# First and final products of field pairs in one pass of 64 by 32 tiles, and a quad's softmax moved beside the next quad's first fields

## The chip, the cores and the metric

The kernel runs on one core of a Trainium2 chip. The metric is the device time in microseconds (us), as the median of several runs. The engines are TensorE (PE, its weight loads PEld), VectorE (DVE), ScalarE (ACT), GpSimd (POOL) and SyncE (SP). Each follows its own list of instructions in order and waits on semaphores for the others.

## The reference

2048 examples have 26 sparse fields, each an index into a table of 12500 rows of 32 numbers, and 13 dense features. All 325 products of two fields' rows are formed, scored by a small attention layer, and pooled with softmax weights:

```python
emb = jax.vmap(lambda tbl, idx: tbl[idx], in_axes=(0, 1), out_axes=1)(embed_tables, sparse)
bi = emb[:, FIRST, :] * emb[:, SECOND, :]                       # 325 pairs x 32
a = jax.nn.relu(jnp.einsum('bpd,dh->bph', bi, att_w_w) + att_w_b)   # 8 hidden
scores = jnp.einsum('bph,ho->bpo', a, att_d_w) + att_d_b
att_weight = jax.nn.softmax(scores, axis=1)
att_out = jnp.sum(att_weight * bi, axis=1)
x = jnp.concatenate([att_out, dense], axis=-1)
out = jax.nn.sigmoid(x @ fin_w + fin_b)
```

The kernel uses that `att_out @ fin_w` is the softmax-weighted sum over pairs of `bi @ fin_w`. So each pair needs two numbers: a score, and a "final" number `bi @ fin_w`.

## The kernel before

The 2048 examples are 4 quads of 4 x 128. Within a quad the loop runs over fields f = 0 to 25.

POOL fetches field rows with indirect transfers (line 431): 4 for each field (2 for field 24, whose other rows SP fetches; none for fields 3, 9, 15 and 19), 86 for a quad, 344 in all. It may start a field of quad q when field f of quad q - 1 has been transposed (line 425), so it may run up to a quad ahead.

Fields 3, 9, 15 and 19 (`LOOK`) are looked up by PE: DVE makes a one-hot matrix (L750), PE multiplies it with the table held in memory (L465, 14 products), and DVE masks and sums the result (L835, L838). Most fields up to 22 have one such look-up beside them, for this quad or the next; the last quad's stop after field 16.

DVE transposes a field (L826), ACT copies the transposed field to PSUM (L651), and DVE multiplies it with all earlier fields (L850). In the last quad DVE itself writes fields 21 to 25 to PSUM (L824). The pairs go, 16 to a group, through a ring of 4 groups; a quad has 21 groups, numbered 0 to 20 here. Groups 15 and 16 end within field 23, group 17 within field 24, groups 18 to 20 within field 25.

For each group PE makes the first products (L482: 4 column tiles of 32, all 128 rows) and, from the same data, the final products (L492). ACT applies relu (L594). Score products (L506) come in batches that end at groups 3, 7, 11, 15, 17 and 20. Sums of scores and of finals gather for 8 groups in a bank each. Then ACT copies a bank to SBUF (L607, L601), PE turns it back (L530, L522), and ACT brings scores and finals home (L622, L613).

Softmax over the first 256 pairs ("early": maximum L890, exponentials L628, sums L895) is done around fields 24 and 25. The rest ("late") follows at the end of the quad: L905 to L945 on DVE and L682 to L687 on ACT. The next quad's first field comes after it. At the very end come the sigmoid and the store.

Of the kernel before, what the change touches and what calls it, by code (L numbers as in the profile page):

```python
# [6 lines left out]
G = 4  # L7
# [4 lines left out]
GROUPS_B = 8  # L12
ROWS_G = P // GROUPS_B
PAIRS_B = GROUPS_B * PAIRS_G
RING = 4
HIDDEN = 6
BATCH = 4
ROWS_SP = 32
# [17 lines left out]
DMA_SCRATCH = 8192  # L36
DIRECT_LAST = 21
# [3 lines left out]
def layout(n_fields, n_dense):  # L41
    at, cols = 0, {}
    for name, width in (("offset", n_fields), ("w", TILE), ("fin", GROUPS_B * TILE), ("d", 2 * TILE), ("bias_a", 1),
                        ("bias_s", 1), ("dense_w", n_dense), ("fin_b", 1), ("ident", P),
                        ("look_chunk", CHUNKS), ("look_row", CHUNK_ROWS)):
        cols[name] = slice(at, at + width)
        at += width
    return cols, at


def attention_fm(nc, dense, sparse, tables, params, look_index, sp_index, chunk_numbers, out):
# [11 lines left out]
    BANKS = -(-GROUPS // GROUPS_B)  # L63
    FULL = BANKS - 1
    LAST = PAIRS - (GROUPS - 1) * PAIRS_G
    LAST_C = -(-LAST // COL_TILES)
    EARLY_PAIRS = FULL * PAIRS_B
    END_GROUPS = GROUPS - FULL * GROUPS_B
# [31 lines left out]
    SHARED_LAST = next(f for f in range(F) if f * (f + 1) // 2 >= (GROUPS_B + 1) * PAIRS_G) - 3  # L100
    look_bank, shared_through = [], []
    for q in range(QUADS):
        for f in range(F + 1):
            for tile in tiles_beside(q, f):
                look_bank.append(1 if f <= SHARED_LAST and look_bank and look_bank[-1] == 0 else 0)
        shared_through.append(max(tile for tile in range(len(look_bank)) if look_bank[tile]) + 1)

    def taken_before(tile):

        return max([t + 1 for t in range(tile) if look_bank[t] == look_bank[tile]], default=0)  # L110

# [10 lines left out]
    assert G * D == P and B % (P * G) == 0 and RING < GROUPS and 1 < END_GROUPS  # L122
# [17 lines left out]
    def groups_of(f):  # L140
# [5 lines left out]
    batch_ends = [gr for gr in range(GROUPS) if gr == GROUPS - 1 or  # L146
                  gr % BATCH == BATCH - 1 and gr < FULL * GROUPS_B or
                  gr == GROUPS - 4]
    assert groups_of(F - 1) == [GROUPS - 3, GROUPS - 2, GROUPS - 1] and groups_of(F - 2) == [GROUPS - 4]
    BATCHES = len(batch_ends)  # L150

# [3 lines left out]
    def place(gr):  # L155

        return gr % BATCH * 2 + gr % GROUPS_B // BATCH


    EARLY_FIELD = 1 + next(f for f in range(F) if FULL * GROUPS_B in groups_of(f))  # L160
    assert EARLY_FIELD < F - 1

    def pairs_c(gr):
        return PAIRS_C if gr < GROUPS - 1 else LAST_C

# [9 lines left out]
    with ctx:  # L175
# [6 lines left out]
        def sem(name):  # L182
# [25 lines left out]
        look_masked = sb("look_masked", [P, D, CHUNK_ROWS])  # L208
        emb_t = sb("emb_t", [P, COPIES, P])
# [3 lines left out]
        hidden = sb("hidden", [P, HIDDEN, PAIRS_C * P])  # L213
        shared = sb("shared", [P, 2 * PAIRS_C * P + 2 * G * WIDTH])
        second_s, second_f = (shared[:, i * PAIRS_C * P:(i + 1) * PAIRS_C * P] for i in range(2))
        score, final = (shared[:, 2 * PAIRS_C * P + i * G * WIDTH:2 * PAIRS_C * P + (i + 1) * G * WIDTH].rearrange(
            "p (g e) -> p g e", g=G) for i in range(2))


        raw_group = {0: 2, 1: 0, 2: 2}  # L220
        raw = [ring[:, raw_group[n]:raw_group[n] + 2].rearrange("p r c j b -> p (r c j b)")[:, 0:PART_ROWS * D]
               if n in raw_group else shared[:, 0:PART_ROWS * D] for n in range(LOOKS)]
# [4 lines left out]
        wrap, moved = (score[:].rearrange("p g e -> p (g e)")[:, i * T * F:(i + 1) * T * F].rearrange(  # L227
            "p (t f) -> p t f", f=F) for i in range(2))
        index_clamped, index_wrap, index_part = (
            final[0:QUADS * LOOKS * G].rearrange("p g e -> p (g e)")[:, G * P + i * P:G * P + (i + 1) * P] for i in range(3))  # L230
        sp_clamped, sp_wrap = (score[0:T].rearrange("p g e -> p (g e)")[:, i * P:(i + 1) * P] for i in range(2))
# [786 lines left out]
```

## Time and profile before

| | |
|---|---|
| time, median of 3 runs | 464.23 us (463.27 to 464.31) |
| time of the profiled execution | 463.98 us, with a span of 462.1 us |
| busy: PE / DVE / POOL / ACT | 398.6 / 395.8 / 333.7 / 129.8 us |
| mean granted TensorE clock | 0.965 of full |

The span is what the profiler shows between the first and the last instruction. The time holds 1.9 us more. Busy shares are averages over stages with different limits. The chain that ended last runs to 47% over POOL's gathers, and another 19% is "issue", nearly all of it between two gathers.

### The profile page before, as it was taken

To read this page: it belongs to the slowest core of one execution; us is meant where nothing else is said; L and a number is where in the kernel's file an instruction comes from. 1 tells how busy PE (TensorE), PEld (TensorE's weight loads), DVE (VectorE), ACT (ScalarE), POOL (GpSimd) and SP (SyncE) were. 2 spreads that over 40 slices of the span, in tenths; PEclk is the share of its full clock that TensorE was granted. 3 is DMA by queue.
4 is the path that set the end of the run, shared out by engine and by line. 5 is a ranking of instruction groups with operands and counts; after the bars stand their busy time and mean duration, and the time that the engine had idled before them with its cause. 6 is when DMAs were issued, how large, how long until landed. Compare 5 with 4: busy or idle time off the path is not lost.

```text
span 462.1 us, 9274 instructions
## 1 busy us (share of the span) xinstructions
PE 398.6 (86%) x2508; PEld 223.6 (48%) x2508; DVE 395.8 (86%) x641; ACT 129.8 (28%) x302; POOL 333.7 (72%) x350
## 2 busy tenths in 40 slices
PE   1686969998898889599988889699989899699894
PEld 0575736553327656244524757354433666434121
DVE  5999797999796978899796998799977898798995
ACT  3303311232252011033252211114235211124363
POOL 5877777777777777777777777777777777777720
PEclk9988879999999999899999999889999999989999
DMA  8467322222112323222212232313211223322210
GB/s 288 99 152 161 28 13 26 17 26 15 14 14 14 37 15 26 14 21 20 18 15 13 26 25 27 14 16 25 16 14 16 15 14 16 13 16 12 17 7 1
DMA packets 16308, 15.44 MB, mean 33 GB/s; under 512 B 7952, under 2 KB 15360, under 8 KB 15872
## 3 DMA queue, kind: packets, MB, share of 16 engines
q0 software_dynamic: 11072, 5.69, 22.9%
q1 hardware_dynamic: 2800, 6.79, 4.2%
q10 hardware_dynamic: 2384, 2.37, 1.7%
q8 instruction: 20, 0.33, 0.3%
q14 instruction: 32, 0.26, 0.2%
HBM read 14.79 MB, written 0.02 MB: 32 GB/s over the span
## 4 chain that ended last, share of the span: by engine, by line
POOL 47%; issue 19%; DVE 15%; PE 14%; DMA 3%; ACT 1%; DVEq 0%; ACTq 0%
POOL emb L431 47%; DVE ring L850 9%; PE first L482 4%; PE sums_f L492 3%; PE looked_own L465 3%; DMA emb<-tables,rows 3%; PE sums_s L506 2%; PE back L465 2%; DVE onehot L750 2%; DVE emb_t L826 1%; DVE look_masked L835 1%; DVE emb L838 1%; DMA ids<-sparse 0%; PE back L530 0%; POOL emb_placed L420 0%
## 5 line engine op out<-in xcount | busy, mean ns | idle before, releaser
L431 POOL DMA_INDIRECT emb<-tables,rows x300 | 283.4, 945 | 91.5 <-issue 90.3
L850 DVE TENSOR_TENSOR ring<-emb_t,turned 128x512 f32<-128x512 f32 (+9 forms) x180 | 191.7, 1100 | 0.3
L465 PE MATMUL looked_own<-look_parts,onehot 128*128 128x448 f32 x546 | 125.7, 383 | 8.7 <-DVE look_masked L835 4.0
L465 PEld LDWEIGHTS looked_own<-look_parts,onehot 128*128 128x128 f32 x546 | 104.3, 196 | 38.4 <-issue 17.7
L482 PE MATMUL first<-ring,par 128*32 128x512 f32 (+1 forms) x672 | 89.0, 607 | 29.7 <-DVE ring L850 29.2
L594 ACT ACTIVATE hidden<-first,par 128x512 f32<-128x512 f32 (+1 forms) x84 | 56.5, 677 | 180.6 <-PE first L482 180.1
L465 PE MATMUL back<-look_parts,onehot 128*128 128x448 f32 x350 | 80.3, 382 | 11.1 <-DVE onehot L750 5.2
L492 PE MATMUL sums_f<-ring,par 128*32 128x512 f32 (+1 forms) x672 | 89.6, 601 | 0.0
L465 PEld LDWEIGHTS back<-look_parts,onehot 128*128 128x128 f32 x350 | 66.4, 195 | 30.8 <-issue 13.3
L750 DVE TENSOR_TENSOR onehot<-chunk_of,turned 128x896 fp32r<-128x896 f16 x60 | 63.2, 1053 | 0.0
L826 DVE STREAM_TRANSPOSE emb_t<-emb 128x128 f32<-128x128 f32 x100 | 29.9, 302 | 35.5 <-DMA emb<-tables,rows 19.7
L431 POOL DMA_INDIRECT emb<-tables,rows_first x44 | 48.2, 1096 | 16.4 <-issue 13.1
L651 ACT ACTIVATE turned<-emb_t 128x128 f32<-128x128 f32 x92 | 25.6, 279 | 103.3 <-DVE emb_t L826 99.5
L482 PEld LDWEIGHTS first<-ring,par 128*32 128x32 f32 x672 | 15.2, 109 | 74.9 <-DVE ring L850 61.8
L492 PEld LDWEIGHTS sums_f<-ring,par 128*32 128x32 f32 x672 | 22.4, 113 | 50.3 <-issue 49.4
L838 DVE TENSOR_REDUCE emb<-look_masked 128x32 f32<-128x448 f32 x64 | 39.7, 620 | 2.2
L506 PE MATMUL sums_s<-hidden,par 128*32 128x512 f32 (+1 forms) x168 | 28.0, 657 | 0.0
L835 DVE TENSOR_TENSOR look_masked<-looked_own,look_mask 128x448 f32<-128x448 f32 x39 | 23.9, 612 | 1.3 <-PE looked_own L465 1.3
L835 DVE TENSOR_TENSOR look_masked<-back,look_mask 128x448 f32<-128x448 f32 x25 | 15.3, 611 | 0.4 <-PE back L465 0.4
L905 DVE COPY shared<-sums_f 128x512 f32<-128x512 f32 x4 | 2.8, 692 | 13.4 <-PE sums_f L492 13.4
L506 PEld LDWEIGHTS sums_s<-hidden,par 128*32 128x32 f32 x168 | 4.9, 117 | 13.8 <-issue 7.2
L756 DVE TENSOR_TENSOR look_parts<-ring,look_parts 128x1792 fp32r<-128x1792 f32 (+1 forms) x6 | 10.5, 1786 | 1.2 <-ACT look_parts L576 1.2
(75 smaller groups left out, 134.9 us busy)
## 6 DMA issues: line engine op xcount, KB each, us to landing
emb_placed<-tables SPq DMA_DIRECT2D x768, 0.1 KB
emb<-tables,rows POOLq DMA_INDIRECT x300, 3.3
ring<-tables SPq DMA_DIRECT2D x2, 1568.0 KB, 7.8
shared<-tables SPq DMA_DIRECT2D x1, 1568.0 KB
chunk_of<-chunk_numbers ACTq DMA_DIRECT2D x12, 128.0 KB, 2.9
ring<-tables SPq DMA_DIRECT2D x1, 896.0 KB, 6.0
emb<-tables,rows_first POOLq DMA_INDIRECT x44, 3.1
ring<-tables SPq DMA_DIRECT2D x1, 672.0 KB, 7.4
```

The lines of the kernel that those rows point to most:

```text
L431: pool.indirect_dma_start(emb[:, f, g * D:(g + 1) * D], None, stacked, bass.IndirectOffsetOnAxis(ap=row, axis=0), element_offset=at,).then ...
L465: mm = nc.tensor.matmul(looked_rows[look_bank[tile]], onehot[:, tile % ONEHOTS, c, :], look_parts[:, n, c, k, :], start=c == 0 and k == 0, ...
L482: mm = nc.tensor.matmul(first[gr % 2][j * TILE:(j + 1) * TILE, 0:n * P], w, ring[:, gr % RING, 0:n, j, :], start=True, stop=True)
L492: mm = nc.tensor.matmul(sums_f[j * TILE:(j + 1) * TILE, 0:pairs_c(gr) * P], row, ring[:, gr % RING, 0:pairs_c(gr), j, :], start=e == 0, st ...
L506: mm = nc.tensor.matmul(sums_s[tile * TILE:(tile + 1) * TILE, cut], d_sel[:, half, :], hidden[:, gr % HIDDEN, cut], start=half == 0, stop= ...
L594: nc.scalar.activation(hidden[:, gr % HIDDEN, cut], first[gr % 2][:, cut], ACT.Relu, bias=par[:, cols["bias_a"]]).then_inc(relu_done, 1)
L651: nc.scalar.activation(turned[f % 2][:, 0, :], emb_t[:, f, :], ACT.Copy).then_inc(turned_made, 1)
L750: nc.vector.tensor_tensor(onehot[:, tile % ONEHOTS], numbers.unsqueeze(1).broadcast_to(shape), here.unsqueeze(2).broadcast_to(shape), ALU. ...
L826: tr = nc.vector.transpose(emb_t[:, f, :], emb[:, f, :])
L835: nc.vector.tensor_tensor(look_masked[:], looked_rows[look_bank[tile]].rearrange("p (i d) -> p d i", d=D), mask, ALU.mult).then_inc(look_m ...
L838: nc.vector.tensor_reduce(emb[:, LOOK[n], g * D:(g + 1) * D], look_masked[:], AX.X, ALU.add).then_inc(look_summed, 1)
L850: nc.vector.tensor_tensor(slot[:, at:at + n, :], emb_t[:, i:i + n, :], turned[f % 2][:, 0, :].unsqueeze(1).broadcast_to((P, n, P)), ALU.mu ...
```

## The change

Each group now gets one set of products, L463 of the new kernel, in place of L482 and L492. The 128 rows are split in two halves of 64 (`ROW_TILES = 2`), and for each of the 4 column tiles there is a product for each half. The 32 columns of a tile hold, for the two of the four blocks that lie in that half, the 8 hidden numbers, the final number and its negative. Both go through relu, and the score products then take relu(x) - relu(-x) for the final. One group thus fills two PSUM banks of three (`FIRST_BANKS = 3`) and needs two relus.

Scores and finals land in one bank `sums`, batch by batch. ACT copies it out, PE turns it back into the same bank, and ACT brings scores and finals home. The next batch's score products wait for that. The ring has 3 groups instead of 4, and the hidden buffer 5 instead of 6. The early maximum of quads 0 to 2 stands behind field 25. The late maximum, the early sums and the late sums of a quad stand beside fields 2, 3 and 6 of the next. The last quad has an order of its own.

```diff
-RING = 4
-HIDDEN = 6
+ROW_TILES = 2
+ROWS_T = P // ROW_TILES
+RING = 3
+HIDDEN = 5
 BATCH = 4
+FIRST_BANKS = 3
...
+LATE_MAX_FIELD, EARLY_SUMS_FIELD, LATE_SUMS_FIELD = 2, 3, 6
+LATE_HOME_FIELD, LATE_EXP_FIELD = 3, 4
...
                 def first_products(gr):
                     pe.wait_ge(pieces_done, q * PIECES + pieces_through_group(gr))
-                    if gr >= 2:
-                        pe.wait_ge(relu_done, q * GROUPS + (gr - 1))
...
+                    if unit(q, gr, ROW_TILES - 1) >= FIRST_BANKS:
+                        pe.wait_ge(relu_done, unit(q, gr, ROW_TILES - 1) - FIRST_BANKS + 1)
                     n = pairs_c(gr)
                     for j in range(COL_TILES):
...
+                        for r in range(ROW_TILES):
+                            rows_r = slice(r * ROWS_T, (r + 1) * ROWS_T)
+                            mm = nc.tensor.matmul(
+                                first[unit(q, gr, r) % FIRST_BANKS][j * TILE:(j + 1) * TILE, 0:n * P],
+                                weights[rows_r],
+                                ring[rows_r, gr % RING, 0:n, j, :], start=True, stop=True)
...
                 def score_products(batch):
...
+                    groups = batch_groups(batch)
+                    pe.wait_ge(relu_done, unit(q, groups[-1], ROW_TILES - 1) + 1)
+                    if q or batch:
+                        pe.wait_ge(final_done, q * BATCHES + batch)
+                        pe.wait_ge(score_done, q * (BATCHES - 1) + batch)
...
+                    for r in range(ROW_TILES):
+                        for e, gr in enumerate(groups):
+                            cut = slice(0, pairs_c(gr) * P)
+                            mm = nc.tensor.matmul(sums[e * TILE:(e + 1) * TILE, cut], d_sel[:, r, :],
+                                                  hidden[:, gr % HIDDEN, r, cut], start=r == 0, stop=r == ROW_TILES - 1,
+                                                  skip_group_check=True)
...
+                def turn_back(batch):
+                    pe.wait_ge(second_done, q * BATCHES + (batch + 1))
                     for c in range(PAIRS_C):
...
+                        mm = nc.tensor.transpose(back[:, c, :], second[batch % 2][:, c * P:(c + 1) * P], ident)
+                    mm.then_inc(back_done, 1)
...
+                    if last and gr == GROUPS - 3:
+                        score_products(BATCHES - 2)
+                        turn_back(BATCHES - 2)
+                    first_products(gr)
...
+                    if q == QUADS - 1 and f == EARLY_FIELD:
+                        copy_second(BATCHES - 2)
+                        homes(BATCHES - 2)
+                        exponentiate_early()
...
+                    if q and f == LATE_MAX_FIELD:
+                        late_maximum(q - 1)
+                    if q and f == EARLY_SUMS_FIELD:
+                        early_sums(q - 1)
+                    if q and f == LATE_SUMS_FIELD:
+                        late_sums(q - 1)
```

PE at the end of the last quad, before: from the products of group 15 on. `first` are first products, `sums_f` finals, `sums_s` scores, and `back` (at the end `first` from `shared`) what is turned back.

```order
L482 MATMUL first<-ring,par 32x512 x4
L522 MATMUL back<-par,shared 128x128 x4
L506 MATMUL sums_s<-hidden,par 32x512 x4
L492 MATMUL sums_f<-ring,par 32x512 x4
L530 MATMUL back<-par,shared 128x128 x4
L482 MATMUL first<-ring,par 32x512 x4
L492 MATMUL sums_f<-ring,par 32x512 x4
L506 MATMUL sums_s<-hidden,par 32x512 x2
L482 MATMUL first<-ring,par 32x512 x4
```

These rows begin with group 16; group 15's pair of rows reads like the two ahead of them. The same place in the new kernel, from the products of groups 14 and 15 (x16) to the end:

```order
L463 MATMUL first<-ring,weights 32x512 x16
L480 MATMUL sums<-hidden,par 32x512 x8
L488 MATMUL sums<-par,shared 128x128 x4
L463 MATMUL first<-ring,weights 32x512 x16
L480 MATMUL sums<-hidden,par 32x512 x4
L488 MATMUL sums<-par,shared 128x128 x4
L463 MATMUL first<-ring,weights 32x512 x16
L463 MATMUL first<-ring,weights 32x256 x8
L480 MATMUL sums<-hidden,par 32x512 x2
```

Batches 3 and 4 (the fourth and the fifth) are each scored and turned back before PE goes on to the next group. Before, one turning back of each kind and batch 3's scores stood between groups 16 and 17, batch 4 (the x2) was scored ahead of group 18, and its turning back came together with batch 5's, behind group 20.

ACT at the same place before, from group 17's relu on: the relus write `hidden`, L628 are the early exponentials, L607 copies out the last scores.

```order
L594 ACTIVATE hidden<-first,par 128x512
L628 ACTIVATE shared,early<-shared,neg_max_early 128x256 x4
L594 ACTIVATE hidden<-first,par 128x512 x2
L594 ACTIVATE hidden<-first,par 128x256
L607 ACTIVATE shared<-sums_s,par 128x512
```

And in the new kernel, from the relus of groups 16 and 17 (x4) on, where L564 copies a bank out and L570 and L576 bring scores and finals home:

```order
L557 ACTIVATE hidden<-first,par 128x512 x4
L564 ACTIVATE shared<-sums,par 128x512
L570 ACTIVATE shared<-sums 128x128
L576 ACTIVATE shared<-sums 128x128
L588 ACTIVATE shared,early<-shared,neg_max_early 128x256 x4
L557 ACTIVATE hidden<-first,par 128x512 x4
L557 ACTIVATE hidden<-first,par 128x256 x2
L564 ACTIVATE shared<-sums,par 128x512
```

The early exponentials and all relus of groups 18 to 20 now stand behind the copy and the homecoming of batch 4.

## Rows read from the trace of the kernel before

**Rows 1.** The page, part 1: busy us of each engine, share, instructions.

```profile
PE 398.6 (86%) x2508; PEld 223.6 (48%) x2508; DVE 395.8 (86%) x641; ACT 129.8 (28%) x302; POOL 333.7 (72%) x350
```

**Rows 2.** Groups by line and form, POOL: busy, mean ns, idle before and its releasers.

```profile
L431 POOL DMA_INDIRECT emb<-tables,rows x300 | 283.4, 945 | 91.5 <-issue 90.3 <-DVE emb_t L826 1.2
...
L431 POOL DMA_INDIRECT emb<-tables,rows_first x44 | 48.2, 1096 | 16.4 <-issue 13.1 <-DVE rows_first L701 3.3
```

**Rows 3.** Timeline of POOL at its end: start, us, engine, line.

```profile
434.09 0.94 POOL L431 DMA_INDIRECT emb<-tables,rows  x1 [0.30 <-issue]
...
441.59 0.94 POOL L431 DMA_INDIRECT emb<-tables,rows  x1 [0.30 <-issue]
```

**Rows 4.** Chain that ended last, in order of time: start, us, what.

```profile
399.14 4.00 DMA emb<-tables,rows
```

**Rows 5.** Waits of DVE between 360 and 462 us: total, times, longest.

```profile
DVE emb_t L826 <- DMA emb<-tables,rows: 4.8, 4, 1.9
DVE emb_t L826 <- ACT turned L651: 2.9, 4, 1.1
```

**Rows 6.** Timeline of DVE around the start of the last quad.

```profile
352.65 0.42 DVE L895 CUSTOM_DVE_ANT_0 shared<-shared 128x256 f32<-128x256 f32 x1
...
359.04 0.69 DVE L905 COPY shared<-sums_f 128x512 f32<-128x512 f32 x1 [3.92 <-PE sums_f L492]
...
365.18 0.31 DVE L826 STREAM_TRANSPOSE emb_t<-emb 128x128 f32<-128x128 f32 x1 [0.35 <-ACT turned L651]
```

**Rows 7.** Timeline of DVE in the last quad's fields 23 to 25.

```profile
438.44 0.32 DVE L824 STREAM_TRANSPOSE turned<-emb 128x128 f32<-128x128 f32 x1
...
446.56 1.22 DVE L890 TENSOR_REDUCE neg_max_early<-shared 128x4 f32<-128x1024 f32 x1 [0.37 <-ACT shared L622]
...
448.04 3.62 DVE L850 TENSOR_TENSOR ring<-emb_t,turned 128x512 f32<-128x512 f32 x3
```

**Rows 8.** Timeline of PE there.

```profile
439.58 1.07 PE L482 MATMUL first<-ring,par 128*32 128x512 f32 x8 [0.88 <-DVE ring L850]
...
443.36 1.07 PE L506 MATMUL sums_s<-hidden,par 128*32 128x512 f32 x8
444.24 1.04 PE L492 MATMUL sums_f<-ring,par 128*32 128x512 f32 x8
...
450.98 1.50 PE L482 MATMUL first<-ring,par 128*32 128x512 f32 x16 [0.27 <-DVE ring L850]
...
455.08 0.66 PE L530 MATMUL back<-par,shared 128*128 128x128 f32 x4 [0.37 <-ACT shared L607]
```

**Rows 9.** Timeline of ACT there.

```profile
440.71 0.69 ACT L594 ACTIVATE hidden<-first,par 128x512 f32<-128x512 f32 x1 [1.97 <-PE first L482]
...
447.81 0.51 ACT L628 ACTIVATE shared<-shared,neg_max_early 128x256 f32<-128x256 f32 x1 [0.17 <-DVE neg_max_early L890]
...
449.92 0.69 ACT L594 ACTIVATE hidden<-first,par 128x512 f32<-128x512 f32 x1
452.12 1.05 ACT L594 ACTIVATE hidden<-first,par 128x512 f32<-128x512 f32 x2 [1.51 <-PE first L482]
454.34 0.69 ACT L607 ACTIVATE shared<-sums_s,par 128x512 f32<-128x512 f32 x1 [1.17 <-PE sums_s L506]
```

**Rows 10.** Groups by line and form.

```profile
L482 PE MATMUL first<-ring,par 128*32 128x512 f32 x640 | 87.3, 618 | 29.7 <-DVE ring L850 29.2
L492 PE MATMUL sums_f<-ring,par 128*32 128x512 f32 x640 | 86.3, 612 | 0.0
...
L506 PE MATMUL sums_s<-hidden,par 128*32 128x512 f32 x160 | 28.0, 670 | 0.0
...
L651 ACT ACTIVATE turned<-emb_t 128x128 f32<-128x128 f32 x92 | 25.6, 279 | 103.3 <-DVE emb_t L826 99.5 <-DVE ring L850 3.4 <-issue 0.3
...
L594 ACT ACTIVATE hidden<-first,par 128x256 f32<-128x256 f32 x4 | 1.9, 465 | 0.0
```

**Rows 11.** Timeline of PE after an idle stretch in the last quad.

```profile
404.91 1.21 PE L482 MATMUL first<-ring,par 128*32 128x512 f32 x8 [4.03 <-DVE ring L850]
```

More of the change, by code:

```diff
@@ L497, in score_products @@
-                def score_products(batch):
-                    first_gr, end = batch_ends[batch - 1] + 1 if batch else 0, batch_ends[batch]
-                    n = first_gr // GROUPS_B
-                    pe.wait_ge(relu_done, q * GROUPS + (end + 1))
-                    if first_gr % GROUPS_B == 0 and n:
-                        pe.wait_ge(second_s_done, q * BANKS + n)
-                    for gr in range(first_gr, end + 1):
-                        tile, half = place(gr) // 2, place(gr) % 2
-                        cut = slice(0, pairs_c(gr) * P)
-                        mm = nc.tensor.matmul(sums_s[tile * TILE:(tile + 1) * TILE, cut], d_sel[:, half, :],
-                                              hidden[:, gr % HIDDEN, cut], start=half == 0,
-                                              stop=half == 1 or gr >= FULL * GROUPS_B, skip_group_check=True)
-                    mm.then_inc(scores_done, 1)
@@ L618, in finals_home, with homes @@
+                def finals_home(batch):
+                    groups = batch_groups(batch)
+                    whole = len(groups) - (batch == BATCHES - 1)
+                    mv = nc.scalar.activation(pairs_of(final_all, groups[0], whole), in_bank(1, slice(0, whole)), ACT.Copy)
+                    if batch == BATCHES - 1:
+                        mv = nc.scalar.activation(end_pairs(final_all), in_bank(1, whole)[:, 0:LAST_C], ACT.Copy)
                     mv.then_inc(final_done, 1)
-                def scores_home(n):
-                    act.wait_ge(back_s_done, q * BANKS + (n + 1))
-                    nc.scalar.activation(pairs_of(score, n * GROUPS_B, GROUPS_B), scores_in_bank(every),
-                                         ACT.Copy).then_inc(score_done, 1)
+                def homes(batch):
+                    scores_home(batch)
+                    finals_home(batch)
@@ L893, in _ @@
-                for g in range(G):
-                    dve.wait_ge(early_exp_done, q * G + (g + 1))
-                    nc.vector.tensor_tensor_reduce(
-                        out=expd[:, g, 0:EARLY_PAIRS], in0=expd[:, g, 0:EARLY_PAIRS],
-                        in1=final[:, g, 0:EARLY_PAIRS], scale=1.0, scalar=0.0, op0=ALU.mult, op1=ALU.add,
-                        accum_out=early[:, 1, g:g + 1]).then_inc(early_num_done, 1)
+                    before = []
+                    if f == 1:
+                        before = tiles_beside(q, 0)[-1:] if q == 0 else tiles_beside(q - 1, F)
+                    elif f:
+                        before = tiles_beside(q, f - 1)
@@ L939, in _ @@
[L939 to L945 removed]
+            early_sums(QUADS - 1)
```

414 lines of the change are left out of this document (193 added, 221 removed).

## The prediction

> **What bounds the kernel now.** The page first: PE and DVE are both at 86% [rows 1], which invites the thought that taking products from PE must pay. The groups by line say otherwise. POOL's 300 later gathers have 283.4 us of work and 91.5 us of gaps, and nearly all of the gaps is "issue": only 1.2 us in all is a wait for another engine [rows 2]. One gather starts every 0.945 + 0.30 = 1.25 us, and 344 of them fill the run to 442.5 us (441.59 + 0.94) [rows 3], of a span of 462.1. So POOL is never held by DVE. An earlier DVE doesn't make POOL earlier.
>
> How closely does the rest follow POOL? The chain shows 4.00 us from the start of a field's last gather to its landing (field 14) [rows 4]. The last gather of field 23 starts at 434.09 [rows 3], so it lands at about 438.1. DVE takes up field 23 at 438.44 [rows 7], 4.35 us after that start. In between DVE has waited for gathers 4 times for 4.8 us in the last quad, and for ACT's copy 2.9 us [rows 5]. So whatever DVE, PE and ACT save in quads 0 to 2 is given back to these waits, and field 23 can come at most 0.3 us sooner. What is left for the change to move is the last 23 us.
>
> **What the change does ahead of that.** PE: it loses 86.3 us of final products [rows 10]. The first products stay at 4 column tiles of 512 columns for each row half. If the halves run beside each other, a group still costs 0.88 us (443.36 to 444.24, one set to the next [rows 8]). Score products double, +28.0 us [rows 10]. PE's sum falls to about 340 us. No row shows two row halves together. The bounds are 0.88 us a group (beside each other) and 1.76 (in turn). I take the first, since four column tiles do share the 0.88 us here. The Trainium skill, "TensorEngine Tiling (Array Packing)", Tiling Modes, lists eight independent tiles of 64 by 32, which would give the same. Its section PSUM Bottleneck warns that a tiled TensorE moves the load to whoever empties PSUM. The trace has nothing on that for row halves; here it means the doubled relus, which stand in the sum below by rows.
>
> ACT: 84 more relus at the 0.585 us pace of back-to-back ones add about 49 us, to some 180 of 462. It has room, but its place in the chain grows.
>
> DVE at the quad changes: before, from the end of field 25's products (352.65) to the third transpose of the next quad (365.18) it took 12.5 us, with 3.92 us of waiting for the finals and 0.35 for ACT in it [rows 6]. The softmax steps that move to fields 2, 3 and 6 are the same work elsewhere, and one bank copy of 0.69 goes. What counts is the waiting. Afterwards DVE waits there for ACT's first copy, which stands behind the end of PE's and ACT's chain. By the parts below that is, from the end of field 25's products: groups 19 and 20 through relu, with the homes of batch 4 between, 3.6; scores 1.95; bank copy 0.7; exponentials 2.1; the copy itself 0.3; in all 8.65. The early maximum of 1.22 [rows 7] lies under it at least, so DVE waits 7.4 us at most, against 4.3. Less the 0.69, it comes at most 2.4 us later to the next fields. The cover is the 4.8 us for which it waits for gathers in the last quad [rows 5]. So I cost this at nothing; without the cover it would be 2.4 us, and once only, as the last quad alone decides the end.
>
> Ring of 3: DVE fills a group in 2.3 us (3.62 for 25 pairs [rows 7], so 0.145 a pair) and may be two ahead of PE, which needs 0.88 us for a group and has more idle time than before. Cost nothing; if it costs some tenths in a field, the gather waits cover them up to field 14.
>
> **The last 23 us, step by step.** Parts: first products to their relu 1.13 (439.58 to 440.71 [rows 8, 9]); a pair of relus 0.585 + 0.69 = 1.28 (the row of 1.05 is one of 512 and one of 256 columns, and the latter is 0.465 [rows 9, 10]); scores of a batch, two passes, 0.88 + 1.07 = 1.95 [rows 8]; bank copy 0.69 [rows 9]; turning back 0.66 [rows 8]; hand-overs 0.03 to 0.05 (454.34 + 0.69 to 455.08 [rows 8, 9]); a home of 128 columns 0.28, as a copy of that size [rows 10], and 0.18 for the next behind it; four early exponentials 2.11 (447.81 to 449.92 [rows 9]).
>
> Group 15 is complete when it was before, since field 23 is: its products start at 439.58.
>
> - Relu pair of 15: 440.71 to 441.99. Scores of batch 3: 442.04 to 443.99. Copy to 444.71, turned back at 445.42. PE does nothing else meanwhile, as its order puts this ahead of group 16, whose pairs lie ready.
> - Group 16 at 445.42, relus 446.55 to 447.83, the first done at 447.24. Group 17 needs that bank: 447.29, relus 448.42 to 449.70.
> - Scores of batch 4: 449.75 to 451.70 (two column tiles at a time, same pace). Copy to 452.42, turned back at 453.13, scores and finals home at 453.61. Then the exponentials, to 455.72. Before, they began at 447.81 [rows 9].
> - Only now ACT comes to relu 18: 455.72, first of the pair done at 456.41. Group 19 at 456.46, relus from 457.59, first done 458.28. Group 20 at 458.33; its 256 columns take 0.62 (1.50 for two sets less 0.88 [rows 8]); its relus 459.0 to 459.84.
> - Scores of batch 5: 459.89 to 461.84, copy to 462.56, turned back at 463.27.
>
> Before, the scores were turned back at 455.74 (455.08 + 0.66 [rows 8]) and the span ended 6.4 us later. The new tail behind that point is the same but for a copy of 128 columns in place of 256, 0.1 us less. So the span becomes 463.27 + 6.3 = 469.5, 7.4 us more, and the profiled time 463.98 + 7.4 = 471.4. The median of 464.23 lies 0.25 above the profiled run; I say 471.5.
>
> DVE isn't what holds this up. Its products of field 25 end at about 451.3 instead of 451.66 (448.04 + 3.62 [rows 7]), as batch 3's scores are home at 445.8, so that the wait of 0.37 ahead of the early maximum goes. That gain of 0.35 us lies beside the chain and is worth nothing.
>
> **The rivals.**
>
> *The row halves run in turn.* The groups 15, 16, 17, 19 and half of 20 in the chain each cost 0.88 more: +3.9, 475.4 us. PE's sum would be 427 us (340 and 87.3 [rows 10]) and the quad changes could add to it. For it: no row shows the halves together. Against it: column tiles do overlap.
>
> *The clock falls in the tail.* After 4.03 us of idle PE, one set took 1.21 us instead of 1.07, in a stretch where the granted clock was at the lower level for a part [rows 11]. The new chain leaves PE waiting for ACT for 2 us and more at a time. If the lower level (1.2 GHz) holds from 456 on, the steps of PE double: 0.9 + 0.6 + 1.95 + 0.6, +4 us, 475.5. Against it: the idle stretches are shorter than 4 us.
>
> *Not slower.* The first 44 gathers take 1.096 us on average, the later ones 0.945 [rows 2]: 6.6 us in which POOL is held, all in the prologue while DVE splits the looked-up tables. The change puts these tables elsewhere and DVE's operations may shift against the gathers. If all of this went, POOL's whole schedule would come 6.6 us earlier, and the end too, 464.8, within measuring. It decides from about 6 us on. Against it: the same eight splittings stand in the same order, so I expect it to move by 1 us either way at most.
>
> *DVE doesn't catch up by field 14.* If the quad change costs 3 us more than counted, field 23 comes up to 2 us late, 473.5.
>
> **How the numbers follow.** The chain as written 0.64, with its own range 469.5 to 473.5 (0.5 us for hand-overs on some twenty steps, 1 us for POOL's floor either way). Halves in turn 0.09, clock 0.10, not caught up 0.07. Not slower 0.10, be it by the prologue or by a tail that I read wrongly. What a measurement of this kernel can tell from no change is 0.3%, or 1.4 us. To be faster by more than that the end would have to come before 462.8: with field 25's last gather at 441.59 and 4 us to land, and then its products and the old tail, the old span could shrink by 2 us at best. So faster 0.04, same 0.06, slower 0.90. The range of 467.5 to 475.7 leaves out the not slower case and the far side of the first two rivals.
>
> **What would show it.** In the new profile: POOL's last gather within 1 us of 441.6; a set of eight first products of 1.1 us, not 2; relu 18 behind the early exponentials at about 455.7, though its products lay ready; batch 3's and batch 4's bank copies at about 444 and 451.7; PE idle between them; DVE waiting for scores at the end for some 8 us. Wrong would be: a POOL that ends much earlier or later, DVE waiting for ACT's copies in every field, or first products of twice the length.

## The result and the profile after

The new kernel takes **480.6 us** (median of 4 runs, 478.55 to 481.8), the kernel before on the same chip 463.75 (463.19 to 464.31). The ratio is 1.0362, 95% interval 1.0341 to 1.0382. It was forecast to be slower, at 471.5 with a range of 467.5 to 475.7. The sign is right and the size isn't: 16.9 us lost where 7.3 were forecast.

The profiled execution took 481.23 us, of which 479.4 are the span. First the page's busy times, the slices of the granted clock, and the groups of the lines that the change touches, the parts that answer to [rows 1, 2, 10]:

```profile
PE 375.4 (78%) x2676; PEld 214.9 (45%) x2676; DVE 399.4 (83%) x638; ACT 185.2 (39%) x414; POOL 334.3 (70%) x350
...
PEclk9888979998799899998799899998799899987576
...
L416 POOL DMA_INDIRECT emb<-tables,rows x300 | 284.8, 949 | 91.5 <-issue 89.7
...
L463 PE MATMUL first<-ring,weights 64*32 64x512 f32 (+1 forms) x1344 | 101.6, 663 | 56.2 <-DVE ring L831 40.2
...
L480 PE MATMUL sums<-hidden,par 128*32 128x512 f32 (+1 forms) x336 | 58.8, 733 | 7.1 <-ACT hidden L557 7.1
...
L845 DVE CUSTOM_DVE_ANT_0 shared<-shared 128x256 f32<-128x256 f32 x16 | 9.0, 609 | 6.5 <-ACT shared L588 6.3
L588 ACT ACTIVATE shared<-shared,neg_max_early 128x256 f32<-128x256 f32 x16 | 11.8, 747 | 0.0
L838 DVE TENSOR_REDUCE neg_max_early<-shared 128x4 f32<-128x1024 f32 x4 | 8.3, 2084 | 1.9 <-ACT shared L570 1.9
```

POOL has the same work and the same gaps. PE has lost 23 us of busy time, less than the 59 forecast (398.6 to 340), and the slices say why in part: the granted clock is below full in far more of them, and at the end it stands at 5 to 7 tenths. The last three rows hold something that the forecast had not: the early softmax's own operations are longer, though their shapes are the same.

Next PE's timeline from the products of group 14 on, to be held against [rows 8]:

```profile
436.88 1.09 PE L463 MATMUL first<-ring,weights 64*32 64x512 f32 x16 [0.35 <-ACT hidden L557]
439.93 1.10 PE L463 MATMUL first<-ring,weights 64*32 64x512 f32 x16 [1.96 <-DVE ring L831]
442.46 3.64 PE L480 MATMUL sums<-hidden,par 128*32 128x512 f32 x16 [1.43 <-ACT hidden L557]
446.91 1.11 PE L488 MATMUL sums<-par,shared 128*128 128x128 f32 x4 [0.81 <-ACT shared L564]
447.95 1.96 PE L463 MATMUL first<-ring,weights 64*32 64x512 f32 x16
450.85 1.96 PE L463 MATMUL first<-ring,weights 64*32 64x512 f32 x16 [0.94 <-ACT hidden L557]
454.23 3.63 PE L480 MATMUL sums<-hidden,par 128*32 128x512 f32 x8 [1.42 <-ACT hidden L557]
458.64 0.66 PE L488 MATMUL sums<-par,shared 128*128 128x128 f32 x4 [0.79 <-ACT shared L564]
459.23 1.09 PE L463 MATMUL first<-ring,weights 64*32 64x512 f32 x16
463.41 1.09 PE L463 MATMUL first<-ring,weights 64*32 64x512 f32 x16 [3.09 <-ACT hidden L557]
465.43 1.11 PE L463 MATMUL first<-ring,weights 64*32 64x256 f32 x16 [0.93 <-ACT hidden L557]
467.52 3.63 PE L480 MATMUL sums<-hidden,par 128*32 128x512 f32 x12 [0.98 <-ACT hidden L557]
471.95 0.66 PE L488 MATMUL sums<-par,shared 128*128 128x128 f32 x4 [0.81 <-ACT shared L564]
```

The order is the forecast one, step for step, and from group 15's relu on PE is idle for ACT alone. The same operation stands here at two durations: a group's products (each of the 8 leaves two records, so x16) in 1.09 and in 1.96 us, turning back in 0.66 and in 1.11. All three score batches run at the long one, 3.63 us, where 1.95 was forecast. ACT in the same stretch, to be held against [rows 9]:

```profile
441.15 1.27 ACT L557 ACTIVATE hidden<-first,par 128x512 f32<-128x512 f32 x2 [1.67 <-PE first L463]
...
446.17 0.69 ACT L564 ACTIVATE shared<-sums,par 128x512 f32<-128x512 f32 x1 [3.76 <-PE sums L480]
...
457.90 0.69 ACT L564 ACTIVATE shared<-sums,par 128x512 f32<-128x512 f32 x1 [3.73 <-PE sums L480]
...
459.67 0.77 ACT L588 ACTIVATE shared<-shared,neg_max_early 128x256 f32<-128x256 f32 x1
...
462.59 1.25 ACT L557 ACTIVATE hidden<-first,par 128x512 f32<-128x512 f32 x2
```

The last row is relu 18. Its products ended at 460.32, and it starts when the early exponentials are through, as forecast, but at 462.59 instead of 455.72. The clock, stretch by stretch, in the kernel before (columns: stretch, its us, busy us and instructions of PE, PE's weight loads, DVE, ACT and POOL, granted clock, DMA share, GB/s):

```profile
425.00:441.00 16.00, 13.56 (x120) 3.03 (x112) 15.25 (x18) 5.34 (x11) 12.04 (x14) 1.00 0.28 15
441.00:458.00 17.00, 14.21 (x122) 4.45 (x114) 14.00 (x30) 10.12 (x27) 1.23 (x2) 1.00 0.06 4
```

and in the new kernel:

```profile
425.00:441.00 16.00, 11.59 (x116) 2.21 (x116) 13.95 (x16) 8.39 (x17) 12.05 (x13) 0.78 0.27 15
441.00:458.00 17.00, 12.26 (x64) 2.34 (x60) 11.34 (x11) 5.24 (x10) 1.88 (x2) 0.50 0.10 5
458.00:472.00 14.00, 7.55 (x65) 1.86 (x65) 2.46 (x8) 7.88 (x18) 0.00 (x0) 0.76 0.00 0
```

Between 441 and 458 the new kernel's TensorE runs wholly at the lower level, 1.2 of 2.4 GHz. It was granted the upper one for all of this in the kernel before.

**Where the time went.** Span 479.4 against a forecast of 469.5, 9.9 us more, of which some 0.3 lie in hand-overs and not in this table:

| term | forecast | measured | more |
|---|---|---|---|
| start of the chain, relu 15 | 440.71 | 441.15 | 0.44 |
| three batches' scores | 3 x 1.95 | 3.64, 3.63, 3.63 | 5.0 |
| groups 16, 17, 20, products to relu | 1.13, 1.13, 0.67 | 2.07, 2.06, 1.20 | 2.4 |
| turning batch 3 back | 0.66 | 1.11 | 0.45 |
| four early exponentials | 2.11 | 2.92 | 0.8 |
| last turning back to the end | 6.3 | 6.8 | 0.5 |

The second to fourth terms, 7.9 us, are the lower clock. The last two, 1.3 us, are the softmax's durations.

DVE's rows tell what it did meanwhile, field 23's first transpose, the early maximum, field 25's products and the wait at the end:

```profile
438.79 0.33 DVE L805 STREAM_TRANSPOSE turned<-emb 128x128 f32<-128x128 f32 x1 [1.25 <-DMA emb<-tables,rows]
...
448.48 1.98 DVE L838 TENSOR_REDUCE neg_max_early<-shared 128x4 f32<-128x1024 f32 x1 [1.94 <-ACT shared L570]
450.73 3.62 DVE L831 TENSOR_TENSOR ring<-emb_t,turned 128x512 f32<-128x512 f32 x3
...
472.65 0.29 DVE L854 COPY shared<-sums 128x128 f32<-128x128 f32 x1 [9.30 <-PE sums L488]
```

Field 23 comes at 438.79, against 438.44 before, and DVE stands idle for 9.3 us at the end.

### The profile page after: what moved, and what is told of

It is laid out like the page before. It is cut to its first block, busy times and chain, and to the rows that moved or that the text cites. A ratio compares the mean times of both kernels' runs of the same rounds, so it can differ in the third digit from the quotient of the medians.

```text
span 479.4 us, 9758 instructions
## 1 busy us (share of the span) xinstructions
PE 375.4 (78%) x2676; PEld 214.9 (45%) x2676; DVE 399.4 (83%) x638; ACT 185.2 (39%) x414; POOL 334.3 (70%) x350
## 4 chain that ended last, share of the span: by engine, by line
DVE 32%; PE 25%; POOL 17%; issue 14%; ACT 7%; DMA 3%; another core or an unknown queue 1%; DVEq 0%; POOLq 0%; ACTq 0%
POOL emb L416 17%; DVE ring L831 14%; PE first L463 10%; PE sums L480 8%; DVE onehot L731 7%; PE looked L446 5%; DVE look_masked L816 4%; ACT hidden L557 3%; DMA emb<-tables,rows 2%; ACT shared L588 2%; DVE emb_t L807 2%; DVE emb L819 1%; DVE shared L845 1%; PE sums L488 1%
## 5 line engine op out<-in xcount | busy, mean ns | idle before, releaser
L446 PE MATMUL looked<-look_parts,onehot 128*128 128x448 f32 x896 | 207.9, 389 | 25.1 <-DVE onehot L731 16.6
L446 PEld LDWEIGHTS looked<-look_parts,onehot 128*128 128x128 f32 x896 | 175.6, 201 | 74.1 <-issue 35.9
L557 ACT ACTIVATE hidden<-first,par 128x512 f32<-128x512 f32 x168 | 104.7, 674 | 155.2 <-PE first L463 154.6
L463 PE MATMUL first<-ring,weights 64*32 64x512 f32 (+1 forms) x1344 | 101.6, 663 | 56.2 <-DVE ring L831 40.2
L480 PE MATMUL sums<-hidden,par 128*32 128x512 f32 (+1 forms) x336 | 58.8, 733 | 7.1 <-ACT hidden L557 7.1
L463 PEld LDWEIGHTS first<-ring,weights 64*32 64x32 f32 x1344 | 16.6, 109 | 102.5 <-DVE ring L831 73.3
L816 DVE TENSOR_TENSOR look_masked<-looked,look_mask 128x448 f32<-128x448 f32 x64 | 39.1, 611 | 0.2
L480 PEld LDWEIGHTS sums<-hidden,par 128*32 128x32 f32 x336 | 12.0, 127 | 51.6 <-issue 33.0
L564 ACT ACTIVATE shared<-sums,par 128x512 f32<-128x512 f32 x24 | 16.5, 688 | 34.4 <-PE sums L480 30.6
L488 PE MATMUL sums<-par,shared 128*128 128x128 f32 x96 | 16.0, 290 | 2.4 <-ACT shared L564 2.4
L838 DVE TENSOR_REDUCE neg_max_early<-shared 128x4 f32<-128x1024 f32 x4 | 8.3, 2084 | 1.9 <-ACT shared L570 1.9
L576 ACT ACTIVATE shared<-sums 128x256 f32<-128x256 f32 (+1 forms) x24 | 8.5, 353 | 1.2 <-DVE shared L855 1.2
```

What stands on the lines that cost most here:

```text
L446: mm = nc.tensor.matmul(looked_rows[tile % 2], onehot[:, tile % ONEHOTS, c, :], look_parts[:, n, c, k, :], start=c == 0 and k == 0, stop=c ...
L463: mm = nc.tensor.matmul(first[unit(q, gr, r) % FIRST_BANKS][j * TILE:(j + 1) * TILE, 0:n * P], weights[rows_r], ring[rows_r, gr % RING, 0: ...
L480: mm = nc.tensor.matmul(sums[e * TILE:(e + 1) * TILE, cut], d_sel[:, r, :], hidden[:, gr % HIDDEN, r, cut], start=r == 0, stop=r == ROW_TI ...
L488: mm = nc.tensor.transpose(back[:, c, :], second[batch % 2][:, c * P:(c + 1) * P], ident)
L557: nc.scalar.activation(hidden[:, gr % HIDDEN, r, cut], first[unit(q, gr, r) % FIRST_BANKS][:, cut], ACT.Relu, bias=par[:, cols["bias_a"]]) ...
L816: nc.vector.tensor_tensor(look_masked[:], looked_rows[tile % 2].rearrange("p (i d) -> p d i", d=D), mask, ALU.mult).then_inc(look_masked_d ...
```

## The experiments

Twelve kernels ran. Each median below goes with its ratio to the kernel before, run beside it. In the diffs, `q == QUADS - 1` is the last quad.

**The new kernel once more.** Its runs spread over some 3 us, so it ran again, unchanged, beside three of the others.

> The changed kernel once more, unchanged, on the chip of the three kernels beside it. Theory: 480.6 within its own spread of about 3 us, which comes from when the lower clock level falls; the profiled run shows at least 10 us of the lower level after 425 us. Rival (the chip or the moment made the 480.6): below 475.

Measured 482.22 us (476.43 to 483.23), ratio 1.0358 (1.0286 to 1.0431). The result holds. PE's rows of its profile have the lower clock in three more places:

```profile
440.01 1.96 PE L463 MATMUL first<-ring,weights 64*32 64x512 f32 x16 [2.79 <-DVE ring L831]
...
459.58 1.11 PE L488 MATMUL sums<-par,shared 128*128 128x128 f32 x4 [0.79 <-ACT shared L564]
460.63 1.96 PE L463 MATMUL first<-ring,weights 64*32 64x512 f32 x16
```

So where the lower level begins and ends differs from run to run, and a spread from 476 to 483 us can come from that: of the eight runs the two shortest, 476.43 and 478.55, have the highest mean granted clock, 0.910 and 0.909, against 0.892 to 0.904 in the others.

**The exponentials later.** This undoes the one step of the order by which ACT's early exponentials stand ahead of relu 18.

```diff
                     if q == QUADS - 1 and f == EARLY_FIELD:
                         copy_second(BATCHES - 2)
                         homes(BATCHES - 2)
-                        exponentiate_early()
...
+                if q == QUADS - 1:
+                    exponentiate_early()
                 copy_second(BATCHES - 1)
```

> One edit to the changed kernel, in the last quad only: the early exponentials stand on ScalarE behind the relus of groups 18 to 20 instead of ahead of them. Theory (the last quad's chain runs through every step of PE and ScalarE in turn): the exponentials held relu 18 for 2.9 us in the changed kernel (459.67 to 462.59); now they lie beside batch 5's scores, which took 3.6 us. So 480.6 - 2.9 = 477.7 us. Rival (VectorE or the gathers set the end, and ScalarE's order is beside it): 480.6, no change.

Measured 479.19 (476.24 to 480.4), ratio 1.0312 (1.0278 to 1.0346): 1.4 us less than the new kernel's first median and 3.0 less than its second. PE's last rows of its profile:

```profile
458.07 1.09 PE L463 MATMUL first<-ring,weights 64*32 64x512 f32 x16 [0.94 <-ACT hidden L557]
460.09 1.03 PE L463 MATMUL first<-ring,weights 64*32 64x256 f32 x16 [0.93 <-ACT hidden L557]
462.06 3.63 PE L480 MATMUL sums<-hidden,par 128*32 128x512 f32 x12 [0.94 <-ACT hidden L557]
466.49 1.11 PE L488 MATMUL sums<-par,shared 128*128 128x128 f32 x4 [0.81 <-ACT shared L564]
```

Relu 18 did start at 457.24, behind its own products and not behind exponentials, and the last turning back is at 466.49 instead of 471.95. This one execution has a span of 474.4, 5.0 less, with a granted clock of 0.84 from 441 to 458. Its mean granted clock is 0.913; the other three executions have 0.899 and take 478.52 to 480.4. The step of the order is as forecast, but its price can't be told apart from where the lower level falls.

**PE kept busy.** The looked-up rows' products of tile 0 are made again and again in the last quad, into a bank that nobody reads by then. The output is whole. The first version puts many of them in, 6 behind the products of groups 9 to 18 and 2 or 3 behind the other steps of the chain.

```diff
+                def fill(n):
+                    if q == QUADS - 1:
+                        for c in range(n):
+                            nc.tensor.matmul(looked_rows[0], onehot[:, 0, c, :], look_parts[:, 0, c, 0, :],
+                                             start=True, stop=True)
...
                         first_products(gr)
+                        if gr >= 9:
+                            fill(6)
...
```

> The changed kernel with products that nobody reads, 2 to 6 of 448 columns at a time, put on PE in the last quad from group 9 on, at the places where PE waits for ScalarE. Theory (what the end took beyond the forecast is TensorE's lower clock level): the granted clock stays at the upper level from 440 to 472 us, the scores of a batch take 1.95 us instead of 3.6, the first products of groups 16 and 17 1.1 instead of 1.96, and the time falls by about 8 us, to 472.6. Rival (the row halves and the two passes are slow by themselves, for instance from changing the tiling): the durations stay and the filler adds up to 1 us a batch, 481 to 484.

Measured 475.3 (473.99 to 476.7), ratio 1.0238 (1.021 to 1.0265). The granted clock was 1.00 from 441 to 458 and the scores took 1.91 us, but the filler stood in the way: relu 15 came at 443.77, and the time is 2.7 us above the 472.6 expected. Hence a second version, with 3 at most places and 2, 4 or 6 at three.

> The changed kernel with fewer unread products than in the first filler run, 2 to 6 at a time, sized so that each set ends before PE's next input is there. Theory (the lower level costs some 8 us of the tail, and the first filler run gave back 3 us by standing in the way): relu 15 starts at about 441.3, the clock stays at the upper level in the tail, 472 to 473.5 us. Rival (5 us is all that the clock was worth): 475 or more.

Measured 474.25 (473.16 to 474.86), ratio 1.0221 (1.0194 to 1.0248): 6.4 us less than the new kernel's first median and 8.0 less than its second, which ran beside it. It is a little above the 472 to 473.5 expected. PE's rows in the chain, the filler left out:

```profile
443.18 1.92 PE L486 MATMUL sums<-hidden,par 128*32 128x512 f32 x16 [0.55 <-ACT hidden L573]
...
445.92 0.66 PE L494 MATMUL sums<-par,shared 128*128 128x128 f32 x4
446.50 1.09 PE L463 MATMUL first<-ring,weights 64*32 64x512 f32 x16
...
451.04 1.91 PE L486 MATMUL sums<-hidden,par 128*32 128x512 f32 x8 [0.60 <-ACT hidden L573]
...
462.21 1.91 PE L486 MATMUL sums<-hidden,par 128*32 128x512 f32 x12 [0.18 <-ACT hidden L573]
...
464.93 0.66 PE L494 MATMUL sums<-par,shared 128*128 128x128 f32 x4
```

and its stretch from 441 to 458:

```profile
441.00:458.00 17.00, 14.55 (x118) 5.88 (x102) 13.94 (x18) 9.40 (x21) 2.33 (x3) 1.00 0.08 5
```

Every one of these steps has the duration of the forecast. The span is 472.4, 2.9 above the forecast 469.5: relu 15 comes 1.16 late (the filler, and field 23's 0.35), the softmax's durations make 1.3, hand-overs 0.4. With the clock given back, the forecast's chain is what the machine does. This settles that the lower clock is the larger part. It doesn't say why the clock fell; the kernel before with narrow finals, below, bears on that.

**The softmax's reads.** Scores and finals are homed as `(e g)`: an exponential or a sum of one of the four row groups reads every fourth f32. Here the same operations read blocks that lie together. The pairs in a block are then the wrong ones, so the output isn't the reference's.

```diff
-        expd = score[:, :, 0:PAIRS]
+        def plane(flat, late):
+            at = EARLY_PAIRS * G
+            cut = flat[:, at:PAIRS * G] if late else flat[:, 0:at]
+            return cut.rearrange("p (g e) -> p g e", g=G)
...
```

> The changed kernel, but the maxima, exponentials and sums of softmax read the same memory in one piece for each block of rows instead of every fourth element. The pairs then belong to the wrong blocks, so the output isn't the reference's; the amount of work is the same. Theory (the interleaved layout costs): the early maximum falls from 2.08 to 1.21 us, an exponential of 256 from 0.75 to 0.50, an early sum from 0.61 to 0.43. In the chain of the last quad stand four exponentials (-0.8) and the late steps (-0.4), so 480.6 - 1.2 = 479.4. Rival (the longer durations come from something else, such as sharing memory with another engine): no change in the durations, 480.6.

The rows that answer to the last three of the page above:

```profile
L593 ACT ACTIVATE shared<-shared,neg_max_early 128x256 f32<-128x256 f32 x16 | 7.9, 499 | 0.0
...
L850 DVE CUSTOM_DVE_ANT_0 shared<-shared 128x256 f32<-128x256 f32 x16 | 6.0, 422 | 3.3 <-ACT shared L593 3.2
...
L843 DVE TENSOR_REDUCE neg_max_early<-shared 128x4 f32<-128x1024 f32 x4 | 4.8, 1211 | 0.0
```

The three durations are back at the kernel before's means of 496, 425 and 1214 ns (singly, the sum 0.42 in [rows 6] and the maximum 1.22 in the forecast), so the layout is their cause, and the tail behind the last turning back is 6.4 us long again, not 6.8. The time was 475.95 (474.46 to 477.01), ratio 1.0249 (1.0225 to 1.0273), 4.6 us less and not 1.2. In its profile the clock was 0.99 from 441 to 458. Whether the shorter operations moved the fall of the clock, or only this kernel's placing of its bursts did, stays open. The 1.3 us of the layout is what its durations say; the rest goes with the clock.

**The softmax at its own quad's end.** The late maximum, the early and the late sums of a quad go back from fields 2, 3 and 6 of the next to the end of their own.

```diff
-                    if q and f == LATE_MAX_FIELD:
-                        late_maximum(q - 1)
...
+                early_sums(q)
+                late_maximum(q)
+                late_sums(q)
```

> The changed kernel with one part undone: late maximum, early sums and late sums of quads 0 to 2 stand at the end of their own quad again, not beside the next quad's first fields. Theory (VectorE catches up with the gathers at about field 14 and again at field 23, with 1.25 us to spare there): each quad change grows by some 4 to 5 us, of which the waits left in the last quad cover 1.5 to 3, so 482 to 484 us. Rival (the place of the softmax is worth nothing, everything is covered by gather waits): 480.6.

Measured 479.6 (478.31 to 482.73), ratio 1.034 (1.0305 to 1.0375). No price, where 482 to 484 was expected: quads 0 to 2 are covered by the gathers wherever the softmax stands. DVE still waited 1.16 us for field 23's rows here, which it took up at 437.81.

**The last quad in the order of the others.** Batch 3 is scored behind the products of group 16 and turned back behind those of group 17, and the early maximum and exponentials come at the end.

```diff
-            return q == QUADS - 1 and gr == EARLY_GROUPS - 1
+            return False
...
-                last = q == QUADS - 1
+                last = False
...
-                        if q < QUADS - 1 and gr == GROUPS - 3:
+                        if gr == GROUPS - 3:
...
-                    if q == QUADS - 1 and f == EARLY_FIELD:
-                        copy_second(BATCHES - 2)
-                        homes(BATCHES - 2)
-                        exponentiate_early()
+                if q == QUADS - 1:
+                    exponentiate_early()
...
```

> The changed kernel with the order of quads 0 to 2 on all engines in the last quad too (first products of the next group ahead of scores and turning back, early maximum behind field 25), and the early exponentials ahead of the last bank copy. Theory (the length of the last quad's chain): by the durations at the upper clock level the last turning back comes at 457.3 us instead of 471.95, and 7 us follow it; with the lower level in part of the tail 2 to 6 us more, so 466 to 471 us. Rival (the chain is long because of what each step costs, not because of their order): 478 or more.

Measured 469.29 (468.13 to 470.1), ratio 1.0107 (1.0072 to 1.0142): the last quad's order was worth 11.3 of the 16.9 us, with what it does to the clock in it. PE's rows:

```profile
443.27 1.96 PE L463 MATMUL first<-ring,weights 64*32 64x512 f32 x16 [0.94 <-ACT hidden L557]
445.16 2.46 PE L480 MATMUL sums<-hidden,par 128*32 128x512 f32 x16
447.55 1.09 PE L463 MATMUL first<-ring,weights 64*32 64x512 f32 x16
...
459.74 0.66 PE L488 MATMUL sums<-par,shared 128*128 128x128 f32 x4 [1.65 <-ACT shared L564]
```

Scores follow on products here without a wait for the relu just asked for. The work is closer together, the clock came back at about 446, and the last turning back is at 459.74 instead of 471.95.

**That order with filler**, 4 unread products behind groups 10, 12, 14, 16 and 20.

> The changed kernel with the order of the other quads in the last one, and with 4 unread products each behind groups 10, 12, 14, 16 and 20 of the last quad. Theory: with the order repaired, of the 469.3 us some 2 to 3 are still the lower level around 440 to 446 (2.46 for a batch's scores, 1.96 for a first set); with the filler 466 to 468. Rival (what is left is not the clock): 469.3.

Measured 467.54 (466.4 to 470.2), ratio 1.0071 (1.0046 to 1.0097). It is the fastest of the kernels that compute all and have the row halves, and still behind the kernel before.

**That order with blocks that lie together** (wrong pairs in a block, as above).

> The kernel with the order of the other quads in the last one, and softmax reading its memory in one piece for each block (pairs in the wrong blocks, so the output isn't the reference's). Theory (the interleaved layout costs only what stands in the tail's chain, the late maximum, late exponentials and late sums, with the early maximum and exponentials beside other work): 468.3 to 469, 0.3 to 1 less than the 469.3 without. Rival (the layout costs 4.6 us, as the first run with it came out): 465.

Measured 467.06 (466.15 to 468.0), ratio 1.0076 (1.0053 to 1.0099), 2.2 less than without. In this profile POOL's last gather also started 2.0 us earlier than in that of the kernel without, so how much of the 2.2 is the reads stays open.

**Is PE the bound before?** The kernel before with finals of 64 columns in place of 512; the other final sums are zero.

```diff
-                        mm = nc.tensor.matmul(sums_f[j * TILE:(j + 1) * TILE, 0:pairs_c(gr) * P], row,
-                                              ring[:, gr % RING, 0:pairs_c(gr), j, :], start=e == 0,
+                        mm = nc.tensor.matmul(sums_f[j * TILE:(j + 1) * TILE, 0:64], row,
+                                              ring[:, gr % RING, 0, j, 0:64], start=e == 0,
...
```

> The kernel before with final products of 64 columns instead of 512, the rest of the bank zero, so that most finals are left out: PE loses some 75 us of work as in the change, and nothing else changes. Theory (the gathers are the floor, PE is not): 464.3, at most 2 us more if the lower clock level comes into the tail. Rival (PE bounds parts of the run): 458 us or less.

Measured 464.79 (463.94 to 465.96), ratio 1.002 (1.0003 to 1.0037). PE's busy time fell from 398.6 to 354.8 us and the time not at all. A shorter PE buys nothing, be it at 86% busy. It also bears on where the lower clock comes from. Its two stretches and the products of group 15:

```profile
425.00:441.00 16.00, 9.63 (x104) 2.95 (x96) 14.29 (x16) 3.58 (x6) 12.04 (x14) 0.77 0.24 15
441.00:458.00 17.00, 12.06 (x126) 4.81 (x118) 13.17 (x25) 9.69 (x23) 1.28 (x2) 0.92 0.06 4
...
439.16 1.93 PE L482 MATMUL first<-ring,par 128*32 128x512 f32 x8 [2.33 <-DVE ring L851]
```

With PE's work cut and all else as before, without row halves and without the new order, the lower level is there too, from about 437.0 to 443.8, next to waits of PE for DVE of 2.71 and 2.33 us. But here it costs the end next to nothing: the span is 462.9 us against 462.1.

**Are the gathers?** Every second gather is left out, in the kernel before and in the new one, and the columns that they would have filled hold constants.

```diff
-                    for g in range(gathers_of(f)):
+                    for g in range(0, gathers_of(f), 2):
...
```

> The kernel before with every second indirect gather left out (those rows hold a constant), so POOL has 172 gathers in place of 344. Theory (the gathers are the floor): the waits for gathers go (19.7 us in all before, and the 9.3 for the placed rows stay), and the end is set by DVE and PE: 435 to 448 us. Rival (the floor is elsewhere): 460 or more.

Measured 441.22 (439.32 to 441.84), ratio 0.9493 (0.9456 to 0.9529). They are the floor, and the next limit is some 23 us below.

> The changed kernel with every second indirect gather left out in the same way. Theory: the change gives DVE nothing either, as its work is the same and it waits for ScalarE's first copy at each quad change, so with the floor gone the changed kernel stays behind by 8 to 16 us. Rival (the freed PE pays as soon as the gathers don't bound): it is faster than the kernel before with half of the gathers.

Measured 466.41 (463.51 to 469.38), ratio to the whole kernel before 1.004 (1.0014 to 1.0065). That is 25.2 us behind the other, more than the 8 to 16 expected. In the two profiles, which are 26.2 us apart, field 23's products start at 427.25 against 416.43, so 10.8 us arise ahead of them and 15.4 in the tail. From the end of field 25's products to the start of the next quad's products of field 14, the three quad changes take 5.2, 5.0 and 4.2 us more than in the kernel before (the rest is 2.1 us less in the first quad and 1.5 less behind field 14 of the last). In the third, field 2's products start 0.7 us sooner (13.8 us after that end, against 14.5), and fields 2 to 14 take 40.0 us against 35.1; the softmax steps that now stand among them take 4.9 us.

## Why the prediction was right in sign and wrong in size

- **"The gathers are the floor": right.** POOL's last gather started at 442.26, 0.67 later than before. Leaving out half the gathers gave the kernel before some 23 us, and 44 us less of PE gave it nothing.
- **"The halves run beside each other": right.** A group's 8 products take 1.09 us, where 4 of 128 rows took as long (a set of 1.07 stands beside [rows 11] in the forecast). Halves in turn would have shown 2 us at the upper clock, and 1.09 also stands in the kernel with light filler, whose clock was 1.00. To what follows on PE it is 1.02 us (434.85 to 435.87), not the 0.88 of the forecast; nothing in the chain hung on that. The Trainium skill's "TensorEngine Tiling (Array Packing)", Tiling Modes, counts eight independent tiles of 64 by 32, and the trace agrees.
- **The order of the chain: right, each step.** Relu 18 behind the exponentials, both batch copies ahead of the next group, PE and ACT in turn, DVE idle for 9.3 us at the end. Undoing the order gave 11.3 us, with what that did to the clock.
- **"Parts" of the last 23 us: the term that was mis-sized, by 7.9 us.** Scores at 1.95, products to relu at 1.13 and turning back at 0.66 are the upper clock's durations, from a stretch of the kernel before in which PE was never long without work. They measured 3.64, 2.07 and 1.11. The clock stood among the rivals instead, from 456 on and at 4 us, with a chance of 0.10 and "the idle stretches are shorter than 4 us" against it. Three things in that were wrong. The lower level came at 441 and not at 456, and it had been there between 425 and 441 as well (clock 0.78). No idle of 4 us was needed: the longest of PE between 425 and the fall at 441 was 1.96 us, and PE was busy for 11.59 of these 16 us. And the rival looked to the chain's waits for ACT, while the clock fell ahead of the chain, whose first step is relu 15 at 441.15; the wait just before the fall was for DVE. What is new in that place is that PE has less to do between DVE's groups, and the kernel before with narrow finals shows such a fall at 437.0 without the chain. There it cost next to nothing. In the chain every step of PE is paid in full. Whether the chain's own gaps also hold the clock down stays open: the lower level stayed for 17 and for 24 us in the new kernel's two profiles, but from 441 to 458 the clock was 0.84 with the exponentials later, 0.87 with the softmax at its quad's end and 0.99 with blocks that lie together, all with the same steps up to batch 4's scores. The light filler, which changes the chain's steps by little and the clock to 1.00, measured the term at 6.4 to 8.0 us.
- **Exponentials of 2.11 us and a tail of 6.3: 1.3 us short.** The durations were taken over from the kernel before because shapes and counts were the same. The diff's `"p (e g) -> p g e"` was there to be read.
- **The quad change "at most 2.4 us": too small.** It was 4.2 to 5.2, by the runs with half the gathers. The forecast counted the waits and took the softmax steps that move for the same work, but the layout makes them longer (four early sums take 2.1 us against 1.4), which is a part of the difference. Costing it at nothing was right all the same, since the gathers covered it, with room left: field 14 of the last quad was used 0.25 us behind its gather's landing (403.8 and 403.55), and DVE still waited 0.70 us for field 22's rows and 1.25 for field 23's. That field 23 came 0.35 late is POOL's doing, whose last gather for it started at 434.77 and not at 434.09.
- **"The prologue": right,** POOL's end moved by 0.67 us.

## What to carry to other kernels

When an edit turns work that overlapped into a chain of two engines, price each TensorE step at both clock levels, not at the durations of the busy stretch it comes from: PE's own part of such a chain may come near doubling, with PE busy for most of the time and no gap above 2 us ahead of the fall (2.8 in the second profile). Taking work from PE can itself bring the lower level, as the kernel before with narrow finals shows, so a saving on PE and a longer chain through PE don't go together well. Before taking a duration over for an operation "that only moves", compare the strides of its operands, not just its shape and count. And an engine at 86% busy is no bound until its waits say so: here 44 us of PE were worth nothing, while the order of the last 20 us was worth 11.

## What the runs showed of the hardware

- Reading every fourth f32 in place of neighbours costs DVE's maximum 2084 ns against 1214, its multiply with sum 609 against 425, ACT's exponential of 256 elements 747 against 496. The Trainium skill, "SBUF — State Buffer", in the section "Door 1: The DMA port swizzle", says that SBUF has lines of 16 bytes and that each access which goes to a new line pays. Four f32 are 16 bytes, so here each access does, and the rows agree that it pays; how much is not on the page. The same passage gives 4 f32 as how far one can stride for free. At a stride of 4 f32 the rows show that it isn't free.
- TensorE's clock was at the lower level for 17 us on end, though PE was at work for 12.26 of them. Unread products behind each step, mostly 3, brought the granted clock from 441 to 458 to 1.00. Narrower products alone, in the kernel before, brought it from 1.00 to 0.77 between 425 and 441.
- Of one and the same kernel the lower level began at 440.9 in one profiled execution and at 439.1 in another, and ended at 458.0 and 463.0. A program whose end hangs on it spreads: 476.4 to 483.2 us in 8 runs, against 462.7 to 465.4 in all runs of the kernel before.
